# Sixteen drains a batch on GpSimd turned into counts, and the attention's query and key parts stored once and read in 4 KB rows

## What is computed

```python
def _layernorm(x, axis=-1, eps=1e-05):
    m = jnp.mean(x, axis=axis, keepdims=True)
    v = jnp.var(x, axis=axis, keepdims=True)
    return (x - m) / jnp.sqrt(v + eps)

def _L1_xattn_ref(target, source, target_mask, source_mask, Wq, bq, Wk, bk, Wv, bv):
    ...                                    # HEADS = 16, HEAD_DIM = 8
    dot = jnp.einsum('bhdt,bhds->bhts', q, k) / math.sqrt(HEAD_DIM)
    mask = target_mask[:, :, :, None] * source_mask[:, :, None, :]
    dot = mask * dot - (1.0 - mask) * NEG
    amap = jax.nn.softmax(dot, axis=-1) * mask
    out = jnp.einsum('bhts,bhds->bhdt', amap, v)
    return out.reshape(b, HEADS * HEAD_DIM, t)

x = x + _L0_xattn_ref(ctx_2048, ctx_2048, _layernorm(x), L0_xattn_ssm_kernel, L0_xattn_D, 8)
x = x + _L0_ffn_ref(_layernorm(x), ...)
x = x + _L1_xattn_ref(_layernorm(x), ctx_2048, mask, mask, L1_xattn_Wq, ...)
x = x + _L1_ffn_ref(_layernorm(x), ...)
```

## Time and profile before

| | |
|---|---|
| median of three runs | 585.58 us (579.73 to 590.35) |
| profiled execution, its time | 580.47 us |
| its span, first to last instruction | 578.7 us |
| TensorE, VectorE, GpSimd, ScalarE busy | 80%, 78%, 65%, 61% |
| mean granted TensorE clock | 0.924 |
| DMA | 54.49 MB, 93935 packets |

### The profile page before, as it was taken

How to read it: one execution, slowest core, us unless ns; L and a number is a source line. 1 busy time by engine, 2 the same in 40 slices (tenths; PEclk the granted TensorE clock), 3 DMA queues, 4 the chain that set the end, 5 groups by cost and what they waited for, 6 DMA issues and landing times.

```text
span 578.7 us, 11242 instructions
## 1 busy us (share of the span) xinstructions
PE 463.3 (80%) x3587; PEld 258.3 (45%) x3587; DVE 453.2 (78%) x885; ACT 350.3 (61%) x607; POOL 377.2 (65%) x692
## 2 busy tenths in 40 slices
PE   1686699997987988888989889898887888777452
PEld 1575477765754544444544344443443333322110
DVE  4586479998669979799899899798988997874341
ACT  1469524333121677788788788788876786776231
POOL 6467389998977757777778778776664762343222
PEclk9888889999879999999899999899999998996755
DMA  6970110101551257357354573546745765210100
GB/s 197 372 174 19 48 28 29 22 7 56 89 120 24 80 79 163 94 99 150 91 102 124 100 144 100 90 120 127 157 103 111 137 143 96 50 24 19 50 9 19
DMA packets 93935, 54.49 MB, mean 94 GB/s; under 512 B 16611, under 2 KB 93603, under 8 KB 93877
## 3 DMA queue, kind: packets, MB, share of 16 engines
q1 hardware_dynamic: 93876, 53.78, 41.0%
HBM read 35.84 MB, written 17.42 MB: 92 GB/s over the span
## 4 chain that ended last, share of the span: by engine, by line
PE 24%; issue 21%; POOL 20%; POOLq 14%; DVE 7%; ACT 6%; DMA 4%; SPq 3%; DVEq 0%; ACTq 0%
PE pair L280 7%; POOL kv L949 5%; PE bank L501 4%; POOL w_raw L1026 4%; ACT cT L1310 3%; POOLq L977 3%; POOLq L42 3%; DVE w_int L1656 2%; POOL w_int L45 2%; POOLq L975 2%; PE pair L488 2%; PE bank L393 2%; PE pair L472 2%; DMA yT<-in_x 2%; POOLq L40 2%
## 5 line engine op out<-in xcount | busy, mean ns | idle before, releaser
L1656 DVE TENSOR_REDUCE w_int<-pair 128x4 f32<-128x1024 f32 x128 | 155.2, 1213 | 28.9 <-PE pair L472 28.3
L1310 ACT ACTIVATE cT<-pair 128x1024 f32<-128x1024 f32 x128 | 131.0, 1023 | 38.2 <-PE pair L488 35.8
L280 PE MATMUL pair<-kv,toep 128*128 128x256 f32 x384 | 102.8, 413 | 11.7 <-POOL kv L949 8.0
L280 PEld LDWEIGHTS pair<-kv,toep 128*128 128x128 f32 x384 | 76.0, 207 | 28.2 <-issue 8.4
L488 PE MATMUL pair<-w_raw,KS 57*128 57x256 bf16 x512 | 51.2, 279 | 33.7 <-ACT cT L1310 23.7
L949 POOL TENSOR_TENSOR kv<-cT 128x512 f32<-128x512 f32 x64 | 66.2, 1041 | 17.9 <-PE pair L280 12.4
L501 PE MATMUL bank<-cT,v_aug 128*32 128x256 f32 x1024 | 73.4, 406 | 0.2 <-ACT qT L1318 0.2
L1481 DVE TENSOR_TENSOR prod<-pair,qT 128x512 f32<-128x512 f32 x64 | 43.8, 685 | 23.5 <-PE pair L280 22.7
L472 PE MATMUL pair<-KS,w_raw 54*128 54x256 bf16 x512 | 50.3, 275 | 11.2 <-DVE w_int L1656 10.8
L488 PEld LDWEIGHTS pair<-w_raw,KS 57*128 57x128 bf16 x512 | 16.9, 95 | 72.9 <-ACT cT L1310 54.1
L1257 ACT ACTIVATE w_raw<-bank,st 128x512 f32<-128x512 f32 x32 | 22.0, 688 | 39.0 <-PE bank L394 39.0
(11 more groups left out here) (174 smaller groups left out, 941.9 us busy)
## 6 DMA issues: line engine op xcount, KB each, us to landing
w_raw<-scr_q SPq DMA_DIRECT2D x32, 192.0 KB
KS<-scr_k SPq DMA_DIRECT2D x32, 192.0 KB
scr_q<-w_int SPq DMA_DIRECT2D x16, 192.0 KB, 2.5
scr_k<-w_int SPq DMA_DIRECT2D x16, 192.0 KB, 2.6
scr_o<-qT SPq DMA_DIRECT2D x64, 36.0 KB
yT<-in_x SPq DMA_DIRECT2D x4, 512.0 KB, 7.6
ctx_all<-in_ctx SPq DMA_DIRECT2D x4, 512.0 KB, 8.1
x_b<-in_x SPq DMA_DIRECT2D x16, 128.0 KB, 4.9
```

The lines of the kernel that those rows point to most:

```text
L280: mm = pe.matmul(bank[:, lh * n:(lh + 1) * n], toep[:, h, (lh - sh) * P:(lh - sh + 1) * P], rhs[:, sh, :], start=(sh == 0), stop=(sh == lh))
L1310: act.activation(probs[g % 4].rearrange("p j l -> p (j l)"), SC[:], ACT.Exp).then_inc(s("scores_free"), 1)
L1656: dve.tensor_reduce(neg_max[:, :, 2 * g:2 * g + 2].rearrange("p t j -> p j t"), M[:].rearrange("p (j t s) -> p j t s", t=KL, s=L), AX.X, A ...
```

## The change

The drains of GpSimd's loop are replaced: each instruction whose result the next needs counts up a semaphore, and GpSimd waits for the count. The instructions and their order stay. The drains of the prologue stay too.

The parts are written once each, six DMAs of 128 rows (query and key, three parts), to one tensor scr_qk, in an order in which the eight heads of a half lie side by side: a row of it is 8 x 256 elements, 4 KB. The loads read such rows; since a run repeats the query part, or steps through the key parts, each run is a DMA, twelve in place of four.

```diff
-    scr_q = nc.dram_tensor("scr_q", [2, P, NT, L], BF16, kind="Internal").ap()
-    scr_k = nc.dram_tensor("scr_k", [2, P, NT, L], BF16, kind="Internal").ap()
+    scr_qk = nc.dram_tensor("scr_qk", [2, 2, 3, 2 * HD, GRP, L], BF16, kind="Internal").ap()
...
-                    pe.wait_ge(s(f"qs{b % 3}_loaded"), 16 * 8 * (b // 3 + 1))
+                    pe.wait_ge(s(f"qs{b % 3}_loaded"), 16 * 16 * (b // 3 + 1))
...
-                first = 0
-                for run in (3, 2, 1):
-                    terms = slice(first, first + run)
-                    sp.dma_start(scr_q[k, :, terms, :], qk_parts[k][:, TERM_Q[first], 0:1, :].broadcast_to([P, run, L])
-                                 ).then_inc(s(f"parts{k}_written"), 16)
-                    sp.dma_start(scr_k[k, :, terms, :], qk_parts[k][:, 0:run, 1, :]).then_inc(s(f"parts{k}_written"), 16)
-                    first += run
+                for t in range(3):
+                    for n in range(2):
+                        sp.dma_start(scr_qk[k, n, t].rearrange("r g l -> g r l"), qk_parts[k][:, t, n, :]
+                                     ).then_inc(s(f"parts{k}_written"), 16)
...
-                stacked = "(g j c) t l -> j (c t) g l"
+                part, row = 2 * HD * GRP * L, GRP * L
                 for j in range(2):
-                    rows = slice(HALF * j, HALF * j + ROWS)
-                    sp.dma_start(QS[n][rows, :, :], scr_q[k].rearrange(stacked, g=GRP, j=2)[j]).then_inc(loaded, 16)
-                    sp.dma_start(KS[n][rows, :, :], scr_k[k].rearrange(stacked, g=GRP, j=2)[j]).then_inc(loaded, 16)
+                    first = 0
+                    for run in (3, 2, 1):
+                        rows = slice(HALF * j + HD * first, HALF * j + HD * (first + run))
+                        q_at = (2 * k * 3 + TERM_Q[first]) * part + HD * j * row
+                        k_at = (2 * k + 1) * 3 * part + HD * j * row
+                        sp.dma_start(QS[n][rows, :, :], bass.AP(scr_qk.tensor, q_at, [[0, run], [row, HD], [1, GRP * L]])
+                                     ).then_inc(loaded, 16)
+                        sp.dma_start(KS[n][rows, :, :], bass.AP(scr_qk.tensor, k_at, [[part, run], [row, HD], [1, GRP * L]])
+                                     ).then_inc(loaded, 16)
+                        first += run
...
+            def split_counted(b, whole, rest, parts, what, last):
+                pool.tensor_copy(parts[0], whole).then_inc(s(f"{what}_split"), 1)
+                pool.wait_ge(s(f"{what}_split"), 3 * b + 1)
+                pool.tensor_tensor(rest, whole, parts[0], ALU.subtract).then_inc(s(f"{what}_split"), 1)
+                pool.wait_ge(s(f"{what}_split"), 3 * b + 2)
+                pool.tensor_copy(parts[1], rest).then_inc(s(f"{what}_split"), 1)
+                pool.wait_ge(s(f"{what}_split"), 3 * b + 3)
+                pool.tensor_tensor(parts[2], rest, parts[1], ALU.subtract).then_inc(s(last), 1)
...
-                pool.drain()
-                pool.tensor_tensor(col(b, out_col), col(b, out_col), half_neg[:, 0:1], ALU.pow)
-                pool.drain()
+                pool.wait_ge(s(f"rstd{n}_steps"), 3 * b + 1)
+                pool.tensor_tensor(col(b, out_col), col(b, out_col), half_neg[:, 0:1], ALU.pow).then_inc(s(f"rstd{n}_steps"), 1)
+                pool.wait_ge(s(f"rstd{n}_steps"), 3 * b + 3)
                 pool.tensor_scalar(dst, src, col(b, out_col + 1), col(b, out_col), ALU.add, ALU.mult).then_inc(s(done), 1)
```

More of the change, by code:

```diff
@@ L756, in write_qk_parts @@
                 if b >= 2:
[L757 to L764 removed]
+                    sp.wait_ge(s(f"qs{(b - 2) % 3}_loaded"), 16 * 16 * ((b - 2) // 3 + 1))
+                for t in range(3):
+                    for n in range(2):
+                        sp.dma_start(scr_qk[k, n, t].rearrange("r g l -> g r l"), qk_parts[k][:, t, n, :]
+                                     ).then_inc(s(f"parts{k}_written"), 16)
             def load_stacked_qk(b):
@@ L970, in _, with normalise @@
                     split_bias()
-            def normalise(b, src, dst, mean, out_col, scale, add, done):
-                pool.tensor_scalar(col(b, out_col), col(b, mean + 1), scale, add, ALU.mult, ALU.add)
-                pool.tensor_scalar(col(b, out_col + 1), col(b, mean), -1.0, 1.0, ALU.mult, ALU.mult)
-                pool.drain()
-                pool.tensor_tensor(col(b, out_col), col(b, out_col), half_neg[:, 0:1], ALU.pow)
-                pool.drain()
+            def split_counted(b, whole, rest, parts, what, last):
[6 more added lines that the diff above has]
+                pool.tensor_tensor(parts[2], rest, parts[1], ALU.subtract).then_inc(s(last), 1)
+            def normalise(b, src, dst, mean, out_col, scale, add, n, done):
+                pool.tensor_scalar(col(b, out_col), col(b, mean + 1), scale, add, ALU.mult, ALU.add
+                                   ).then_inc(s(f"rstd{n}_steps"), 1)
+                pool.tensor_scalar(col(b, out_col + 1), col(b, mean), -1.0, 1.0, ALU.mult, ALU.mult
+                                   ).then_inc(s(f"rstd{n}_steps"), 1)
+                pool.wait_ge(s(f"rstd{n}_steps"), 3 * b + 1)
+                pool.tensor_tensor(col(b, out_col), col(b, out_col), half_neg[:, 0:1], ALU.pow).then_inc(s(f"rstd{n}_steps"), 1)
+                pool.wait_ge(s(f"rstd{n}_steps"), 3 * b + 3)
                 pool.tensor_scalar(dst, src, col(b, out_col + 1), col(b, out_col), ALU.add, ALU.mult).then_inc(s(done), 1)
@@ L985, in normalise_x1 @@
                     pool.wait_ge(s("xqT_filled"), b - 1)
-                normalise(b, x1[b % 2], xq[b % 2], MEAN1, RSTD1, 1.0, LN_EPS, "xn1_ready")
+                normalise(b, x1[b % 2], xq[b % 2], MEAN1, RSTD1, 1.0, LN_EPS, 1, "xn1_ready")
             def add_output_bias(b):
@@ L1009, in scale_parts @@
                     pool.wait_ge(s("sh_ready"), b - 1)
[L1010 to L1017, removed]
+                pool.tensor_copy(s6[k][:, 0:3], col(b, SX).broadcast_to([P, 3])).then_inc(s("scale_steps"), 1)
+                pool.tensor_scalar(col(b, SG), col(b, QX), gammas[:, 0:1], 0.5, ALU.mult, ALU.mult).then_inc(s("scale_steps"), 1)
+                pool.wait_ge(s("scale_steps"), 5 * b + 1)
+                pool.tensor_tensor(col(b, R0), col(b, SX), s6[k][:, 0:1], ALU.subtract).then_inc(s("scale_steps"), 1)
+                pool.wait_ge(s("scale_steps"), 5 * b + 2)
+                pool.tensor_scalar(col(b, KAPPA), col(b, QX), gammas[:, 1:2], col(b, SG), ALU.mult, ALU.mult
+                                   ).then_inc(s("scale_steps"), 1)
+                pool.wait_ge(s("scale_steps"), 5 * b + 3)
+                pool.tensor_copy(s6[k][:, 3:5], col(b, R0).broadcast_to([P, 2])).then_inc(s("scale_steps"), 1)
+                pool.wait_ge(s("scale_steps"), 5 * b + 5)
                 pool.tensor_tensor(s6[k][:, 5:6], col(b, R0), s6[k][:, 3:4], ALU.subtract).then_inc(s("s6_ready"), 1)
@@ L1040, in normalise_x2 @@
                     pool.wait_ge(s("qk_bank_ready"), b)
-                normalise(b, x2[:, b % 6, :], xn2, MEAN2, RSTD2, 1.0, LN_EPS, "xn2_ready")
+                normalise(b, x2[:, b % 6, :], xn2, MEAN2, RSTD2, 1.0, LN_EPS, 2, "xn2_ready")
             def split_qk(b):
@@ L1049, in split_qk @@
                     pool.wait_ge(s(f"parts{k}_written"), 16 * 6 * (b // 2))
-                split3(pool, qk, qk_rest, [qk_parts[k][:, n, :, :] for n in range(3)]).then_inc(s("qk_parts_ready"), 1)
+                split_counted(b, qk, qk_rest, [qk_parts[k][:, n, :, :] for n in range(3)], "qk", "qk_parts_ready")
             def split_maxima(b):
@@ L1057, in split_maxima @@
                     pool.wait_ge(s("nm_T_ready"), b)
-                split3(pool, neg_max.rearrange("p t (g j) -> p t j g", j=2),
-                       nm_rest.rearrange("p t (g j) -> p t j g", j=2), [nm_parts[:, :, :, n, :] for n in range(3)]
-                       ).then_inc(s("nm_parts_ready"), 1)
+                split_counted(b, neg_max.rearrange("p t (g j) -> p t j g", j=2),
+                              nm_rest.rearrange("p t (g j) -> p t j g", j=2), [nm_parts[:, :, :, n, :] for n in range(3)],
+                              "maxima", "nm_parts_ready")
             def add_attention(b):
@@ L1066, in add_attention @@
                 pool.wait_ge(s(f"o_nat{k}_loaded"), 32 * (b // 2 + 1))
-                pool.tensor_tensor(o_nat[k], o_nat[k], o_den[k], ALU.mult)
-                pool.drain()
+                pool.tensor_tensor(o_nat[k], o_nat[k], o_den[k], ALU.mult).then_inc(s("attention_scaled"), 1)
+                pool.wait_ge(s("attention_scaled"), b + 1)
                 pool.tensor_tensor(x3[b % 3], x2[:, b % 6, :], o_nat[k], ALU.add).then_inc(s("x3_ready"), 1)
@@ L1074, in normalise_x3 @@
                 pool.wait_ge(s("var3_ready"), b + 1)
-                normalise(b, x3[b % 3], xr[b % 3], MEAN3, RSTD3, 1.0 + RMS_EPS, RMS_EPS * LN_EPS, "xr_ready")
```

(1 more changed line is left out.)

## The result

The changed kernel takes 672.8 us (median of 4 runs, 668.9 to 674.1) where the kernel before, beside it and with one run more than in the table above, took 583.3 (4 runs, 579.7 to 590.4): 1.155 times as long, 95% interval 1.145 to 1.164. The profiled execution spans 670.9 us at a mean granted clock of 0.873; before it was 578.7 us at 0.924.

What follows compares the result with a forecast made beforehand. Waits between engines, mostly through GpSimd until about 390 us, were taken as the bound. 580.5 + 35.5 (TensorE waiting for loads) - 3.5 (drains) - 5 (relief) = 607.5, forecast as a median of 610 us, range 576 to 640.

Steps and rivals of the forecast that it cites:

- case 1: Stacked loads run on few engines and land late, so TensorE waits: 610 us, own range 597 to 634, chance 0.64.
- Drains: GpSimd's loop: each replaced drain gains 0.07 us; 83 before 224 us give 3.5 us, those after nothing beyond the relief.
- the second case: Stacked loads not confined, using all 16 engines: only the drains count, 12 us gained, median 571 us, chance 0.13.
- case 4: GpSimd's own counts cost more than drains: up to 10 us more, 620 to 630 us, chance 0.04.
- Writes at nothing: Six writes per batch to scr_qk: 96 rows on each of 8 engines, the same as before, costed at nothing.
- The two engines, shared by all narrow loads; 68 rows; 0.153 us each: Stacked loads: the first two engines each carry 68 rows of 4 KB at 0.153 us, 10.4 us per batch.
- Cases 2, 3 and 5: Loads: 2, not confined, 571 us, 0.13; 3, narrow on different engines, 576 to 588, 0.12; 5, slow rows, 840, 0.07.
- Leaves 1.8: Stacked loads: what a transfer takes besides its rows, 1.8 us, read from the last load of the maxima.
- L: Time from SyncE's issue of a batch's first stacked load to the loads' landing: 10.4 plus 1.8, 12.2 us.
- N minus T: From a batch's first stacked load issue (T) to TensorE's first product reading it (N): 123.1 us over batches 3 to 15.
- I take a quarter, 5 us: From one batch's N to the next T: late TensorE lets GpSimd get ahead, 5 us gained out of 0 to 19.
- It ends before the rows do: SyncE: issuing twelve loads takes up to 6 us against 2 before, but ends before their rows, so adds nothing.

Runs made afterwards that it cites:

- e1: The kernel before with only GpSimd's drains replaced by counts, writes and loads as before: 570.0 us, 0.982 of before.
- e2: The changed kernel with the drains put back, so only the new writes and loads: 678.0 us, 1.165 of before.
- e4: The changed kernel with 40 filler products on TensorE ahead of the wait for the loads, batches 3 to 15: 653.6 us, 1.126 of before.
- e3: The changed kernel with the dimension of size 8 outermost in the source of the loads of runs: 591.9 us, 1.021 of before.
- e5: The changed kernel with the 8 outermost only in the loads of j = 1, the second half of the heads: 614.0 us, 1.057 of before.

## Why the direction was right and the size wrong

The forecast was 610 us with a range to 640; it was 672.8. The mechanism is that of case 1, "narrow and late": the waits are where they were foretold (before L471, 14 of them), and the DMA share after T is 0.13 to 0.21 in the windows shown and 0.20 to 0.23 over six microseconds (said: 0.13 to 0.19). Step by step:

- **Drains.** 0.07 us each: right, the gaps in the splits shrank by 0.06 to 0.07. The 12 us that the second case gives to the drains alone came out as 11.5 in e1. The place fits only in part: of the 12.5 us between the two profiled executions 7.4 are won by N of batch 9 and 5 after it, where hardly any were expected. The 3.5 us by N of batch 2 can't be told from the spread: e1 is there 4.2 us before the kernel before, the kernel after 2.3 us before e2, and e4, whose code up to there differs from the kernel after only in the order of two waits of TensorE, 3.2 us before that.
- **Counts that cost more than drains** (case 4). Ruled out by e1.
- **Writes at nothing.** No run has the new writes alone, so what they cost on the wire stays open. They hold SyncE for 3.8 us in most batches (3.7 to 4.6) instead of 3.2, and stand in e3's chain.
- **The two engines, shared by all narrow loads; 68 rows; 0.153 us each.** Right, all three: the share right after T, the slope of 0.149 between this kernel and e5, and e3 without confinement. Cases 2, 3 and 5 fall with it.
- **"Leaves 1.8", the fixed part of L.** Here the sum failed first. L was 12.2; measured, N minus T averages 14.8 (192.4 / 13). Taking 68 rows at 0.15 off leaves 4.6 us that are not rows at their steady rate. The packet records name part of it, as means of batches 3 to 15. The first row starts 1.55 us after T in nearly all batches, and not at once. The rows start in threes, one for each of the three engines, as I read it; the first two rows of an engine take 0.9 us together where two later ones take 0.3; one of them alone takes up to 1.1 (25 GB/s in 468.40 to 469.40 us, 66 from 472 on). From the last row's end to the product there are 0.5. Of the 1.8 us that are left the records show only that 17 to 33 of a batch's later rows take over 0.2 us where most take 0.16. I had taken the 1.8 from a load within the chip's own memories, whereas these read a DRAM tensor, and had no row for how such a transfer begins. Why the first rows and some later ones are slow was not tried. This is 2.6 x 13 = 34 us: with it the predicted 35.5 becomes 69, the measured growth of N-T.
- **"I take a quarter, 5 us", the relief in T-N.** It was to fall by 5 and rose by 21.5. The prediction has no term for what a wait does to TensorE afterwards. After waits of 4 to 6.6 us TensorE goes on at the lower level for part of the time (a mean of 0.58 over the next 6 us). The filler gave back 15.8 of the 21.5. What e4 leaves over e1 is 5.4 us, and e3, with hardly any wait, has 8.3. SyncE's longer issue is the likely cause, by e3's chain; but both also run at a lower clock than e1 (0.968 and 0.938 against 1.000 from N of batch 2 to N of batch 15), so the split is not shown.
- **"It ends before the rows do", the issue of twelve DMAs.** True for the kernel after, where the rows take longer still. Without confinement issue leads the chain, at 7.4 us for the loads instead of "up to 6". Case 2 said that all engines at work would give 571; e3 with 8 engines gives 592. The wrong part there is, by e3's chain, the cover: the attention write and the maxima's load stand behind 11 to 12 us of issue, and "shift with it" was counted as free.
- **Iterations after 400 us of 22 to 23 us:** 25.8 between batches 12 and 13, before 19.7, for the same reasons.

The sum with the measured terms: 580.5 + 2.7 (N of batch 2) + 69.3 + 21.5 - 1.3 = 672.7, the time of the profiled execution. The prediction had -3.5, 35.5 and -5 for the first three. It left batches 0 to 2 out as covered, but in batch 2 N minus T is already longer (15.1 against 12.3), with a wait of 3.6 us. So the direction was right by its reasons, and the size missed half of the growth in N-T and the sign of T-N.

What stays open: the slow first rows, the 1.8 us behind them, and how the 5 to 8 us of T-N divide between the loads' issue, the writes' issue and the clock.

## What to carry to other kernels

Read which dimension of a DMA's pattern is outermost before counting its bytes: the same rows cost 81 us more here with 3 and 2 outermost than with 8, and rows of 4 KB instead of 512 B did not make up for it. Count the issues as well, 0.3 to 0.8 us each for these shapes on a queue that other transfers stand in; here cutting four loads into twelve cost 2.7%. When a change makes TensorE wait, add the price of the clock afterwards: look at the granted clock in a window behind each wait, and try filler products to see how much of a loss is clock.

Of the two halves of this change the counts are worth keeping: e1 runs in 570 us where before takes 581.

## What the runs showed of the hardware

- A wait on GpSimd's own semaphore leaves a gap of 0.06 to 0.09 us, a drain 0.12 to 0.14, in the splits; 256 of them replaced gained 1.8% (e1).
- The issue of one load on SyncE depends on its pattern: 0.31 to 0.47 us in most batches for the four of before, 0.60 to 0.79 for a source of [3, 8, 2048] or [2, 8, 2048] against 24 or 16 partitions, 0.28 to 0.46 for a single part. Which property of the pattern makes the difference was not tried.
- Loads confined to 3 and to 2 engines, issued one after the other, pile up on the same ones: 0.13 to 0.23 of 16 in use with several under way, and 0.149 us more for each 4 KB row on the fullest engine (kernel after against e5).
- In the kernel after, the first two rows of an engine take 0.9 us together (mean of batches 3 to 15), later ones mostly 0.16 each.
- The granted clock in the 6 us behind a wait for the loads: 0.50 to 0.73 after the 13 waits of 4.27 to 6.56 us in the kernel after. In e5, 0.50 to 0.94 after the five waits of 3.20 to 4.42 us; after the eight of 0.71 to 2.20 us it was 1.00 seven times and 0.72 once (after 1.78). In e3, 0.72 after 2.39. So the length of the wait alone does not tell which it will be.
